# Each edge product as four 64 by 64 quadrant products in a graph-convolution kernel

## What is computed

```python
xn = layernorm(x)
# graph part
msgs = edge_val[:, None] * xn[src]                     # 212,500 x 256
agg = segment_sum(msgs, dst, num_segments=12500)
support = (1.0 + eps) * xn + agg
gnn = relu(support @ W1.T + b1) @ W2.T + b2
# "mix" part: qkv products, batchnorm, linear attention per node, projection (row by row here)
x = x + gnn + mix(xn)
# feed-forward part, 256 -> 1024 -> 256, kept for the rows chosen by a router
x = x + ffn(layernorm(x))
```

## Time and profile before

| | |
|---|---|
| time, median of 3 runs | 2632.83 us (2632.32 to 2636.76) |
| the profiled execution's own time | 2637.63 us |
| its span, first to last instruction | 2636.0 us |
| mean granted TensorE clock | 0.983 of full |
| busy, share of span: PE / PEld | 94% / 82% |
| busy, share of span: DVE / ACT / POOL | 69% / 56% / 67% |
| main loop (about 216 to 2507 us) | 2291 us, 49 steps |

### The profile page before, as it was taken

The page is one execution under the profiler, slowest core; times in us unless marked ns, Lnnn a source line. Parts: engine busy times, 40 slices in busy tenths (PEclk is TensorE's granted clock), DMA queues, the critical chain, the costliest instruction groups (busy, mean ns, idle before and its releaser), DMA issues.

```text
span 2636.0 us, 42907 instructions
## 1 busy us (share of the span) xinstructions
PE 2489.5 (94%) x12654; PEld 2172.5 (82%) x12654; DVE 1806.4 (69%) x5986; ACT 1464.7 (56%) x3513; POOL 1753.3 (67%) x1858
## 2 busy tenths in 40 slices
PE   5688899999999999999999999999999999999997
PEld 4466688888888888888888888888788888888886
DVE  5754676767767677776776867667676776777657
ACT  4453555655556565565655556556565655656531
POOL 0006777777777777777777777777777777777600
PEclk9798999999999999999999999999999999999998
DMA  7433444344444444434344444443434444343338
GB/s 228 153 115 88 119 118 127 114 121 124 120 125 115 120 124 120 125 116 128 115 121 123 117 126 114 121 123 115 126 115 126 118 121 121 111 129 114 108 116 278
DMA packets 195537, 333.37 MB, mean 126 GB/s; under 512 B 47839, under 2 KB 138013, under 8 KB 195209
## 3 DMA queue, kind: packets, MB, share of 16 engines
q0 software_dynamic: 85216, 233.60, 31.1%
q1 hardware_dynamic: 105018, 92.42, 10.9%
q10 hardware_dynamic: 5072, 4.57, 0.6%
HBM read 291.99 MB, written 38.46 MB: 125 GB/s over the span
## 4 chain that ended last, share of the span: by engine, by line
PE 76%; DVE 9%; ACT 6%; DMA 6%; issue 2%; ACTq 1%; POOL 1%; SPq 0%; DVEq 0%; POOLq 0%
PE bank L1168 23%; PE qkv L1263 13%; PE bank L1275 12%; PE bank L1182 9%; PE bank L1212 6%; PE qkv L1192 4%; DMA work<-in_x 4%; PE qkv L1191 2%; PE bank L1228 2%; PE bank L1237 2%; PE bank L1202 2%; DVE rings L975 2%; DMA rings<-xn_dram,window 1%; DVE work L407 1%; ACT work L465 1%
## 5 line engine op out<-in xcount | busy, mean ns | idle before, releaser
L781 POOL DMA_INDIRECT rings<-xn_dram,window x1764 | 1740.5, 987 | 651.3 <-issue 381.4
L1168 PE MATMUL bank<-rings 128*128 128x256 f32 x3528 | 891.9, 381 | 28.1 <-DMA rings<-xn_dram,window 16.3
L1168 PEld LDWEIGHTS bank<-rings 128*128 128x128 f32 x3528 | 654.6, 190 | 130.2 <-DVE rings L975 32.8
L975 DVE TENSOR_SCALAR rings<-iota,window_dst,window 128x128 f32<-128x128 f32 x1764 | 559.8, 364 | 150.3 <-PE bank L1168 136.2
L1263 PE MATMUL qkv<-work,ffn_weights 128*128 128x256 f32 x1568 | 362.9, 380 | 0.0
L1275 PE MATMUL bank<-ffn_weights,work 128*128 128x256 f32 x1568 | 362.0, 379 | 0.0
L871 ACT ACTIVATE work<-qkv,fb 128x256 f32<-128x256 f32 x392 | 159.6, 472 | 310.5 <-PE qkv L1263 309.9
L1275 PEld LDWEIGHTS bank<-ffn_weights,work 128*128 128x128 f32 x1568 | 297.2, 190 | 40.0
L1263 PEld LDWEIGHTS qkv<-work,ffn_weights 128*128 128x128 f32 x1568 | 293.9, 190 | 37.8
L1182 PE MATMUL bank<-resident,weights 128*128 128x256 f32 x1176 | 279.0, 381 | 0.0
L1182 PEld LDWEIGHTS bank<-resident,weights 128*128 128x128 f32 x1176 | 224.5, 191 | 30.7
(11 more groups left out here) (222 smaller groups left out, 3332.5 us busy)
## 6 DMA issues: line engine op xcount, KB each, us to landing
rings<-xn_dram,window POOLq DMA_INDIRECT x1764, 2.8
xn_dram<-work SPq DMA_DIRECT2D x14, 896.0 KB, 7.7
work<-xn_dram SPq DMA_DIRECT2D x49, 256.0 KB, 3.1
work<-in_x SPq DMA_DIRECT2D x48, 256.0 KB
out<-work SPq DMA_DIRECT2D x48, 256.0 KB
work<-in_x SPq DMA_DIRECT2D x13, 896.0 KB, 5.9
rings<-out SPq DMA_DIRECT2D x6, 896.0 KB, 8.6
out<-rings SPq DMA_DIRECT2D x6, 896.0 KB, 6.8
```

The lines of the kernel that those rows point to most:

```text
L781: nc.gpsimd.indirect_dma_start(out=msg[q][:, :], out_offset=None, in_=xn_dram[:, :], in_offset=bass.IndirectOffsetOnAxis(ap=window[t % WIN ...
L975: v.tensor_scalar(sel[k % SEL_RING], iota[:, :], window_dst[b][:, k % SLOTS:k % SLOTS + 1], window[b][:, k % SLOTS, 2:3].bitcast(F32), ALU ...
L1168: te.matmul(agg[h][:, 0:D], sel[k % SEL_RING], msg[q], start=first, stop=last, skip_group_check=True).then_inc(slot_used, 1)
```

## The change

The product of a slot is done as four products. Quadrant (r, e) takes rows 64r to 64r+63 of `sel` and `msg` (64 edges) and columns 64e to 64e+63 of `sel` (64 destinations), all 256 columns of `msg`, and is placed on the quadrant (64r, 64e) of the array. The halves r = 0 and r = 1 are added up in different banks, `agg[0]` and `agg[1]`. Each bank now holds both tiles of a step: tile h in columns 256h to 256h+255. So `take_sup` reads both banks, in two DVE instructions with a semaphore between them, and the first slot of every tile waits for the reading of the tile just before it. `take_sup` of tile 0 is moved from k=27 to k=17 in DVE's table.

```diff
+        sup_half = sem("sup_half")
-        DVE_AT = dict(scale=(5, 10), out=(6, 13), c=(12, 18), ft=(14, 29), sup=(27, 0), n4=1, f=4, y=5, x=3,
+        DVE_AT = dict(scale=(5, 10), out=(6, 13), c=(12, 18), ft=(14, 29), sup=(17, 0), n4=1, f=4, y=5, x=3,
...
-                v.scalar_tensor_tensor(sup[h], xnin[h], eps1_col, agg[h][:, 0:D], ALU.mult, ALU.add
-                                       ).then_inc(sup_ready, 1)
+                v.scalar_tensor_tensor(sup[h], xnin[h], eps1_col, agg[0][:, h * D:(h + 1) * D], ALU.mult, ALU.add
+                                       ).then_inc(sup_half, 1)
+                dve.wait_ge(sup_half, 2 * i + h + 1)
+                v.tensor_tensor(sup[h], sup[h], agg[1][:, h * D:(h + 1) * D], ALU.add).then_inc(sup_ready, 1)
...
-                    te.matmul(agg[h][:, 0:D], rem_sel[:, :], rem_msg[:, :], start=False, stop=False,
+                    te.matmul(agg[0][:, h * D:(h + 1) * D], rem_sel[:, :], rem_msg[:, :], start=False, stop=False,
...
                 if first:
-                    after(pe, sup_ready, i * 2 + (h - 1))
+                    after(pe, sup_ready, i * 2 + h)
...
-                te.matmul(agg[h][:, 0:D], sel[k % SEL_RING], msg[q], start=first, stop=last,
-                          skip_group_check=True).then_inc(slot_used, 1)
+                for r in range(2):
+                    for e in range(2):
+                        rows_, cols_ = slice(64 * r, 64 * r + 64), slice(64 * e, 64 * e + 64)
+                        ins = te.matmul(agg[r][cols_, h * D:(h + 1) * D], sel[k % SEL_RING][rows_, cols_], msg[q][rows_],
+                                        start=first, stop=last, skip_group_check=True, tile_position=(64 * r, 64 * e))
+                ins.then_inc(slot_used, 1)
```

## The result

The changed kernel takes 3206.36 us (median of 4 runs, 3201.84 to 3209.09) against 2633.18 us: ratio 1.217, 95% interval 1.215 to 1.219. It is slower, as forecast, but by 573 us and not by 1274. The range held it; the likeliest case did not. The profiled execution took 3204.7 us, with a span of 3203.1 us, 567 us over that of before.

A forecast was written before the change was run, and what follows sets the result against it. TensorE, busy 94% of the span, was taken as the bound. To 2637.6 us came 760 (slots), 159 (run tails), 243 (switches) and 157 (slot 18), less 45 of old waits: 3912, as median 3907 us; range 2880 to 4680.

The forecast's parts named there:

- the likeliest case: Pairs of matmuls start in list order across the quadrants: 3907 us, own range 3660 to 4220, chance 47%.
- The pitch of a slot: Edge matmuls on TensorE: four steps of 0.216 us, 0.863 us a slot, 0.431 us more than before.
- The terms of 760 and 159 us: TensorE: 760 us for slower slots over 1764 slots, 159 us for the last matmul's tail in 735 runs of slots.
- The switch: TensorE going between quadrants and whole array: 1470 times at 0.165 us, +243 us, between 0 and 400.
- The wait at slot 18: TensorE waits there until DVE has read tile 0: 3.2 us in each of 49 steps, +157 us.
- the rival's 4.8 us: Wait at slot 18 per step if quadrants overlap fully and each switch costs 0.165 us.
- The clock: Half rate for 6 us after the slot 18 wait each step: +147 us; all slots at half, 5430 us; chance 5%.
- The old waits: Waits of today in TensorE's main loop, taken away by a longer step: -45 us.
- The rival of full overlap: Slots still cost 0.431 us; only slot 18 waits and switches add: 2892 us, or 3071 with paid switches; chance 20%.
- The weight loads: Loads of a slot's eight matmuls stay hidden on TensorE; rival that they show: 4290 to 4670 us, chance 13%.

The follow-up runs named there:

- e4: e3 with each quadrant's product split into two of 128 columns that follow each other in the list; 2918.39 us, ratio 1.108.
- e5: e3 with an already met wait on each of the four products of a slot; ratios 1.072 and 1.073 on two of the slower chips.
- e2: Kernel before, with each slot done as two products of 64 columns, banks, waits and places unchanged; 2827.8 us, ratio 1.074.
- e1: Changed kernel with whole-array products instead of quadrants, slots in turn in the two banks; 3032.96 us, ratio 1.153.
- e8d: Changed kernel with tile 0 read at DVE's place 15 instead of 17, on a chip with the usual time before; 3129.98 us, ratio 1.188.
- e3: Changed kernel with tile 0 read at DVE's place 13 instead of 17; 2860.71 us, ratio 1.086.
- e6d: e1 with tile 0 read at DVE's place 13, on a chip with the usual time before; 2694.05 us, ratio 1.024.

## Why the prediction was right or wrong

**The pitch of a slot: wrong, and this is the step that failed.** "TensorE takes its list in order, so the first matmul of the next quadrant can start beside the second one of this quadrant, but not before it" gave 0.863 us a slot. It is 0.431 (48 matmuls in 2.75 us with one switch). The terms of 760 and 159 us both fall: together 919 us for nothing. e4 and e5 show that the inference from list order was the fault: blocks of four matmuls on one quadrant cost 0.04 us more a slot where list order would have cost 0.9, and in e5 the first matmuls of four products start before any second one. No row of before had two matmuls on different parts of the array, so a list order read from the code stood in for a measurement.

**The switch: right.** 243 us, in the sum at 0.165 us each. Measured are 231 us of busy time, 0.33 us a pair of switches, and 191 to 205 net of old waits. The number of runs was wrong: `PE_AT` names 15 slots, but steps without feed-forward work have fewer, so there are 702 runs and not 735. The time per switch was the middle of three values that no row supported, so its closeness is in part luck. The Trainium skill's rule in "TensorEngine Tiling (Array Packing)", Key Properties, that changing the mode drains TensorE, agrees: the price is the difference between duration and pitch, and e2 pays it for column halves as well.

**The wait at slot 18: the mechanism right, the size set by the wrong branch.** DVE's 6.2 us from `mix_ft`'s reading to the end of `take_sup` were measured as 6.2. The sum took 3.2 us a step, for TensorE slowed by its slots; with fast slots the rival's 4.8 us was the nearer one, and measured are 5.2 (251 us in 48 waits), and 6.0 in e1, where 6.1 was worked out. In the step shown `mix_ft` ended at 1512.85 and DVE read it only at 1514.40: DVE was late by its own list, and did not wait for `mix_ft` as the sum had it. At slot 0, where the forecast put about 1 us in seven steps and left it in the range, there are 8 waits of 17 us together.

**The clock: a rival at 147 us inside the range.** It fell around the wait in every step that had one at slot 18, and cost 94 to 108 us. It was left out of the likeliest sum, though the earlier trace rows had shown it.

**The old waits: partly right.** 45 us were to go, and 28 went: the wait for ACT at the qkv products fell from 18.4 to 2.7 us and that for DMA from 16.3 to 1.7, but the one for DVE's selection matrices stayed (10.7, now 12.8). With the 9 us at L1220, which the earlier trace rows leave out, some 39 went.

**The rival of full overlap** said 3071 us with paid switches, and with the 147 us of the clock 3218; measured 3206. It had 20%. Its mechanism is the one that the runs show, but so close a number is luck in part: the clock was some 40 us less than in it and the waits were 33 us more. What the Trainium skill says in "TensorE: Matmul & The Clock Gate", Measured speedup vs the span model, of starts a few ns apart on different tiles, is borne out here: four matmuls start some 7 ns apart, and the second matmuls of the pairs likewise. I had set what its section The mechanism says of matmuls that keep program order above that; the rows of e4 and e5 go against taking it as a bound for the pairs of float32 products.

**The weight loads** stay hidden, as forecast: with 24 matmuls in 1.45 us, one switch included, there is no room for them on the path.

## What to carry to other kernels

Splitting a full float32 product over quadrants of the array gained nothing here, where the whole array was already used: the pitch of a slot stayed at 0.43 us, and every change between split and whole work cost about 0.17 us. If it is to be done, put the split products in few long runs. Before sharing a PSUM bank between two accumulations, look where in the reader's list the read can stand, since a late read was paid here as a wait (251 us at slot 18) and then once more as half clock (94 to 108 us).

## What was not expected

- Matmuls in the order of four pairs, each pair on one quadrant, ran four at a time: 0.431 us a slot; in e4, with 16 passes in blocks of four, 0.47.
- TensorE gaps of 4.1 us brought 1.2 GHz every time (e8d), gaps of 2.1 to 2.5 us ten times of twelve (e3, e6d), and 47 gaps of 0.5 us never (e6d).
- In one and the same program (e5) the eight matmuls of a slot start in different orders, by when the products arrive.
- The same kernel took 2633 us on some chips and 3033 to 3048 us on three others, with stalls on ScalarE and TensorE in the traces taken on these three for which no cause is recorded. This stays open.
